# A hybrid attention, SSD and expert layer: the order of low parts, exponentials and output copies in attention, and the place of W_out's product

## The reference

```
x = x + attention(layernorm(x))     # 16 heads of 32, causal, softmax, Wo
x = x + experts(layernorm(x))       # 8 experts of rank 16, the best 2 by softmax gates
x = x + ssd(layernorm(x))           # below
x = x + experts(layernorm(x))       # the same weights

ssd(u):  proj = u @ W_in.T  -> xBC, z, A_log ; xBC = causal convolution of 4 taps over tokens + conv_b
         x, B, C = split(xBC) ; a = -softplus(A_log) ; L = exp(segsum(a))     # 32 heads of 16, state 64
         y = (C B^T * L) x + D x ; out = (y * silu(z + z_bias)) @ W_out.T
```

## Time and profile before

| | us |
|---|---|
| median of 3 runs (lowest, highest) | 3169.89 (3167.56, 3171.26) |
| the profiled execution, its time | 3168.84 |
| the profiled execution, its span | 3167.1 |

### The profile page before, as it was taken

How to read it: one execution, slowest core, us unless ns; L and a number is a source line. 1 busy time by engine, 2 the same in 40 slices (tenths; PEclk the granted TensorE clock), 3 DMA queues, 4 the chain that set the end, 5 groups by cost and what they waited for, 6 DMA issues and landing times.

```text
span 3167.1 us, 58505 instructions
## 1 busy us (share of the span) xinstructions
PE 2895.3 (91%) x20788; PEld 2064.0 (65%) x20788; DVE 1943.5 (61%) x2910; ACT 1181.2 (37%) x1877; POOL 696.5 (22%) x997
## 2 busy tenths in 40 slices
PE   3888989999898899999988889999989889999998
PEld 3655477777665457777765545777776544777776
DVE  2545465777745555677765556377776444647777
ACT  2244334444124423444323441444422443244442
POOL 3300012333210001333311001133322000023331
PEclk7999999999999999999999999999999999999999
DMA  9322011111232202111133220211123230111112
GB/s 342 84 60 65 18 52 49 46 50 47 82 73 59 58 14 54 46 48 49 41 94 74 48 48 14 67 49 48 38 68 88 48 78 18 42 50 51 46 45 77
DMA packets 163781, 192.03 MB, mean 61 GB/s; under 512 B 43963, under 2 KB 103995, under 8 KB 161787
## 3 DMA queue, kind: packets, MB, share of 16 engines
q1 hardware_dynamic: 156126, 175.57, 20.5%
q10 hardware_dynamic: 7456, 13.90, 1.4%
HBM read 106.99 MB, written 23.36 MB: 41 GB/s over the span
## 4 chain that ended last, share of the span: by engine, by line
PE 69%; DVE 13%; issue 8%; ACT 4%; SPq 3%; DMA 3%; POOL 1%; ACTq 1%; DVEq 0%; POOLq 0%
PE ps L745 14%; PE ps L746 13%; PE ps L747 13%; DVE mneg L1648 5%; PE ps L1110 4%; PE ps L993 3%; PE ps L923 3%; PE ps L866 3%; PE ps L1096 2%; PE ps L908 2%; PE ps L1119 2%; PE ps L1156 2%; PE ps L861 2%; ACT PR L1298 1%; DMA win_raw<-in_t 1%
## 5 line engine op out<-in xcount | busy, mean ns | idle before, releaser
L745 PE MATMUL ps<-uh,win 128*128 128x512 f32 x1536 | 625.4, 407 | 18.1 <-POOL win L1893 17.4
L746 PE MATMUL ps<-ul,win 128*128 128x512 f32 x1536 | 603.3, 393 | 0.0
L747 PE MATMUL ps<-uh,win 128*128 128x512 f32 x1536 | 602.0, 392 | 0.0
L1648 DVE TENSOR_REDUCE mneg<-ps 128x1 f32<-128x896 f32 (+7 forms) x512 | 366.9, 752 | 274.6 <-PE ps L866 273.1
L1298 ACT ACTIVATE PR<-ps 128x1024 f32<-128x1024 f32 (+3 forms) x384 | 293.3, 808 | 334.0 <-PE ps L908 307.2
L745 PEld LDWEIGHTS ps<-uh,win 128*128 128x128 f32 x1536 | 289.8, 189 | 92.8 <-POOL win L1893 19.8
L747 PEld LDWEIGHTS ps<-uh,win 128*128 128x128 f32 x1536 | 289.8, 189 | 64.9
L746 PEld LDWEIGHTS ps<-ul,win 128*128 128x128 f32 x1536 | 290.6, 189 | 53.8
L1762 DVE TENSOR_TENSOR LM<-ps,LM 128x512 f32<-128x512 f32 x256 | 170.2, 686 | 242.4 <-PE ps L1110 198.4
L1973 POOL TENSOR_SCALAR_AFFINE_SELECT LM<-LM 128x512 f32<-128x512 f32 x256 | 209.5, 830 | 491.4 <-ACT LM L1401 491.4
L923 PE MATMUL ps<-PR,V 128*32 128x512 f32 (+3 forms) x1536 | 285.9, 497 | 3.6 <-ACT PR L1298 2.3
(11 more groups left out here) (220 smaller groups left out, 5039.8 us busy)
## 6 DMA issues: line engine op xcount, KB each, us to landing
raw<-in_t SPq DMA_DIRECT2D x128, 256.0 KB, 2.8
QS<-EV SPq DMA_DIRECT2D x192, 128.0 KB, 2.5
KS<-EV SPq DMA_DIRECT2D x168, 128.0 KB, 2.6
in_t<-tiles ACTq DMA_DIRECT2D x10, 1024.0 KB, 9.2
XN<-in_L_attn_a_x_dram SPq DMA_DIRECT2D x40, 256.0 KB, 5.1
win_raw<-in_L_attn_a_Wqkv_dram SPq DMA_DIRECT2D x34, 256.0 KB, 3.4
win_raw<-in_t SPq DMA_DIRECT2D x32, 256.0 KB, 2.7
edec<-ed_t SPq DMA_DIRECT2D x512, 16.0 KB, 1.6
```

Of the source, the lines that this page charges most:

```text
L745: pe.matmul(dst, hi_l, hi_r, start=first, stop=False)
L746: pe.matmul(dst, hi_l, lo_r, start=False, stop=False)
L747: return pe.matmul(dst, lo_l, hi_r, start=False, stop=last)
L1648: dve.tensor_reduce(mneg[:, hh, t:t + 1], flat[:, off:off + (t + 1) * P], AX.X, ALU.max, negate=True).then_inc(a_max.sem, 1)
```

## The change

In attention, VectorE runs `project_lo` behind both groups of maxima of a session, not between them. ScalarE runs the exponentials of the next pair's units 0 and 1 ahead of `take(p, g, hf, 1)`. In a pair's first session TensorE issues the scores of units 2 and 3 one by one, each with its own wait. The load of W_out is issued after y of pair 13 is saved, ahead of pair 15's decays; its high part is made inside pair 14; the low part is split, half on VectorE inside pair 14 and half on GpSimd at the start of pair 15. The products of tiles 0 to 3 with k = 0 to 2 stand in four places inside the last pair (`fill`), those of tiles 5, 6, 4, 7 after it, each tile with a bank of its own; the parts k = 3 of all tiles come last. The last gate tile is done in two halves of tokens, each with a signal, and the last y is saved by SP and ScalarE, two transfers each. Ten matmuls of no use (`keep_awake`) stand behind the product.

```diff
@@ SP
-                    def save_y(j, q):
+                    def save_y(j, q, chunks):
...
-                        for c4 in range(4):
+                        for c4 in chunks:
...
-                                elif q == 2:
-                                    bc_pe.wait(sp, b * PAIRS + j, 2)
-                                    sp.dma_start(wout_raw, wout_dram.rearrange("p (k n) -> p k n", k=KT)).then_inc(s_wout, 16)
...
-                                save_y(j, q)
+                                save_y(j, q, range(2) if last and q == 3 else range(4))
+                                if last and q == 1:
+                                    bc_pe.wait(sp, b * PAIRS + j + 1, 2)
+                                    sp.dma_start(wout_raw, wout_dram.rearrange("p (k n) -> p k n", k=KT)).then_inc(s_wout, 16)
                                 if not (last and q >= 2):
                                     pair_decay(j + 2, q % 2)
@@ TensorE
                             if ahead:
                                 group_scores_a(p + 1, pair + 1, FILLING[k][0])
-                            scores_b(p, pair, (2 * k + 2, 2 * k + 3))
+                            if k == 0:
+                                scores_b(p, pair, (2,))
+                                scores_b(p, pair, (3,))
+                            else:
+                                scores_b(p, pair, (2 * k + 2, 2 * k + 3))
...
+                def product_part(t, k):
+                    t0 = t * P
+                    return three(ps[:, t, :], gh[:, k, t0:t0 + P], gl[:, k, t0:t0 + P], woh[:, k, :], wol[:, k, :], k == 0, k == KT - 1)
+
+                def product_start(t):
+
+                    for k in range(KT - 1):
+                        product_part(t, k)
...
+                    def fill(t):
+                        if ahead is None:
+                            if t == 0:
+                                gate.wait(pe, b, KT - 1)
+                                for i in range(2):
+                                    wout_lo[i].wait(pe, b, 1)
+                            if t == 2:
+                                bc_dve.wait(pe, n, 2)
+                            product_start(t)
...
                     segment(0)
                     project_ahead(0, 1)
+                    fill(0)
...
                     i.then_inc(ds_pe.sem, 1)
+                    fill(1)
                     inner(0)
                     segment(1)
...
                     project_ahead(1, 0)
+                    fill(2)
                     segment(2)
                     segment(3)
                     inner(1)
                     project_ahead(1, 1)
+                    fill(3)
...
-                wout_lo.wait(pe, b, 1)
-                row_product(lambda dst, k, t0, first, end:
-                            three(dst, gh[:, k, t0:t0 + P], gl[:, k, t0:t0 + P], woh[:, k, :], wol[:, k, :], first, end),
-                            b * 2 + 1, lambda: gate.wait(pe, b, KT - 1), lambda: gate.wait(pe, b, KT))
+                for t in (5, 6, 4, 7):
+                    if t == 4:
+                        y_dve.wait(pe, b * PAIRS + PAIRS - 1, 1)
+                    product_start(t)
+                for t in range(TT):
+                    if t % HALF == 0:
+                        gate.wait(pe, b, KT + t // HALF)
+                    product_part(t, KT - 1).then_inc(w_pe.sem, 1)
+                w_add.wait(pe, b * 2 + 1, 1)
+                keep_awake(0, 10)
+                w_add.wait(pe, b * 2 + 1, TT - 2)
@@ ScalarE
-                        take(p, g, hf, 1)
                         if ahead:
                             for u in range(2):
                                 exponentials(p + 1, u)
+                        take(p, g, hf, 1)
...
                     if later is not None:
                         pair_hi(n + 2, par, later)
+                    elif ahead:
+                        wout_split()
...
-                            if last and par == 0:
-                                wout_split()
                 value_hi(b + 1)
+                y_dve.wait(act, b * PAIRS + PAIRS - 1, 1)
+                for c4 in range(2, 4):
+                    act.dma_start(yt[3 * 32:4 * 32, :].rearrange("p (a c l) -> p a c l", a=2, c=4)[:, :, c4, :],
+                                  y1[c4 * 32:(c4 + 1) * 32, :, :]).then_inc(s_ysave, 16)
@@ VectorE
-                                    if g < GROUPS - 1 and k < 4:
-                                        project_lo(g + 1, k, False)
+                            if hf == 0 and g < GROUPS - 1 and k < 4:
+                                project_lo(g + 1, k, False)
...
                     if later:
                         pair_lo(n + 2, par)
+                    elif ahead:
+                        wout_hi.wait(dve, b, 1)
+                        dve.tensor_tensor(wol[:, 0:2, :], wout_raw[:, 0:2, :], woh[:, 0:2, :].bitcast(F32), ALU.subtract).then_inc(wout_lo[0].sem, 1)
...
-                            if last and q == 2:
-
-                                wout_hi.wait(dve, b, 1)
-                                dve.tensor_tensor(wol, wout_raw, woh[:, :, :].bitcast(F32), ALU.subtract).then_inc(wout_lo.sem, 1)
...
-                add_tiles(b * 2 + 1, w_pe, w_add, 0, b * 4 + 3, X)
+                add_tiles(b * 2 + 1, w_pe, w_add, 0, b * 4 + 3, X, banks=TT)
@@ GpSimd
+                    if final:
+                        pool.tensor_tensor(wol[:, 2:KT, :], wout_raw[:, 2:KT, :], woh[:, 2:KT, :].bitcast(F32), ALU.subtract).then_inc(wout_lo[1].sem, 1)
                     until(ya_pe, n, 0)
...
+                            if last and par:
+                                until(wout_hi, b, 1)
+                            mix(n, j, par, last and par)
```

More of the change, by code:

```diff
@@ L264, in hybrid_layer @@
         wout_hi = signal("wout_hi", 1)
-        wout_lo = signal("wout_lo", 1)
+        wout_lo = [signal(f"wout_lo{i}", 1) for i in range(2)]
         ln_var = signal("ln_var", 2)
@@ L366, in hybrid_layer @@
         s_zero = sem("s_zero")
-        gate = signal("gate", KT)
+        gate = signal("gate", KT + 1)
         SIGNALS_OF = {
-            "vector": [wout_lo, bcw_lo, ln_var, ln_xh, ln_lo, v_done, w_add, pj_lo, a_max, o_rec, z_dve, g_in, g_w, u_add,
+            "vector": [wout_lo[0], bcw_lo, ln_var, ln_xh, ln_lo, v_done, w_add, pj_lo, a_max, o_rec, z_dve, g_in, g_w, u_add,
                        al_dve, a_dve, cm_dve, cm_low, ed_in, xz_dve, bc_dve, scan, m_dve, y_mid, y_dve, gate],
@@ L373, in hybrid_layer @@
                        bt_act, cm_act, ed_act, ds_act, dt_act, seg_act],
-            "gpsimd": [wv_lo, qkw_lo, xzw_lo, ln_rstd, *o_scaled, cp_pool, xd_pool, xp_pool, sel_pool, st_pool],
+            "gpsimd": [wout_lo[1], wv_lo, qkw_lo, xzw_lo, ln_rstd, *o_scaled, cp_pool, xd_pool, xp_pool, sel_pool, st_pool],
             "tensor": [ln_tp, v_pe, w_pe, pj, a_pe, m_pe, st_pe, pv, z_pe, t_pe, u_pe, al_pe, dc_pe,
@@ L927, in weigh, with keep_awake @@
                     i.then_inc(pv.sem, 1)
-                def keep_awake(bank):
-                    for _ in range(4):
+                def keep_awake(bank, n=4):
+                    for _ in range(n):
                         pe.matmul(ps[:, bank, :], onesr[:, :], uh[:, 0, 0:HB], start=True, stop=True)
@@ L1496, in by_tile, with add_tiles @@
                         take(t - 1)
-            def add_tiles(n, product, added, bank, stats_of, src, loaded=None):
+            def add_tiles(n, product, added, bank, stats_of, src, loaded=None, banks=4):
                 for t in range(TT):
                     product.wait(dve, n, t + 1)
-                    dve.tensor_tensor(X[:, t, :], ps[:, bank + t % 4, :], X[:, t, :], ALU.add).then_inc(added.sem, 1)
+                    dve.tensor_tensor(X[:, t, :], ps[:, bank + t % banks, :], X[:, t, :], ALU.add).then_inc(added.sem, 1)
                     if t >= 1:
@@ L1798, in gate_tile, with tile @@
                     one = slice(m, m + 1) if isinstance(m, int) else bass.ds(m, 1)
-                    def tile(a):
-                        return a[:, one, :].rearrange("p a t -> p (a t)")
-                    xm, zm = tile(xT), tile(zs)
-                    at = (b * KT + m) * 3
-                    dve.scalar_tensor_tensor(xm, xm, dsk[:, one], yt, ALU.mult, ALU.add).then_inc(s_gate, 1)
-                    dve.wait_ge(s_gate, at + 1)
-                    dve.tensor_tensor(zm, xm, zm, ALU.mult).then_inc(s_gate, 1)
-                    dve.wait_ge(s_gate, at + 2)
-                    dve.sem_inc(s_tick, 1)
-                    dve.tensor_copy(tile(gh), zm).then_inc(s_gate, 1)
-                    dve.wait_ge(s_gate, at + 3)
-                    dve.tensor_tensor(tile(gl), zm, tile(gh).bitcast(F32), ALU.subtract).then_inc(gate.sem, 1)
+                    halves = 2 if isinstance(m, int) else 1
+                    for half in range(halves):
+                        tok = slice(half * L // halves, (half + 1) * L // halves)
+                        def tile(a):
```

(17 more changed lines are left out.)

## The result

| | before | after |
|---|---|---|
| median of 4 runs each, us | 3168.72 (3166.48 to 3171.26) | 3111.56 (3107.40 to 3118.52) |
| the profiled execution, its span | 3167.1 | 3110.5 |
| VectorE, share of the span | 61% | 62% |
| granted TensorE clock, mean | 0.977 | 0.980 |

The ratio is 0.9822, 95% interval [0.9802, 0.9841]: 57.2 us faster, where 50 to 51 were forecast. The time lies 7 us under the forecast and inside its range.

A forecast was written before the change was run, and what follows sets the result against it. TensorE was taken to bound the kernel, its idle time largely waits for VectorE's maxima. The terms 38.4 - 3.6 + 10.6 + 5.7 = 51.1 us gave 3118.5 us, 1.6% faster; range 3106 to 3142.

The forecast's parts named there:

- Low parts: Attention sessions: maxima start earlier with the low part behind them, 0.80 us at each of 48 waits, 38.4 us.
- stack copies: Attention: QS and KS copies, released later, make TensorE wait 0.9 us in the third group, 3.6 us cost in all.
- Exponentials and split: Attention's changes of pair: exponentials ahead of output copies, scores 2 and 3 apart; 2.6 us per image, 10.6 in all.
- step 2: Sign in attention: L904's waits for exponentials fall to some 5 us outside the last pair; output-copy waits stay small.
- W_out: Last SSD pair to expert logits: 36 matmuls moved inside the pair, some 2.7 us per image gained, 10.9 us before clock loss.
- step 3: W_out inside the last pair; signs: VectorE without gaps from first sum, 37 to 38 us to logits, half clock in first logits.
- The clock: First expert logits behind W_out: TensorE falls to half clock, 1.3 us lost per image, -5.2 us in all.
- A: Whole kernel: everything fits, stack copies land in time and the clock holds in the tail; 3110 us, chance 0.22.
- B: Attention: waits move to stack copies, an exponential or bank 7, losing half the low parts' gain; 3138 us, chance 0.11.
- C: Attention: maxima still released by something as late, so the low parts gain nothing; 3153 us, chance 0.05.
- D: Attention: late stack copies stall 12 places, 5 us each, making the kernel slower by 0.2% (6 us); chance 0.04.

The follow-up runs named there:

- wout_only: Kernel after with both attention edits undone, so only what concerns W_out is changed against the kernel before: 3162.02 us, ratio 0.9977 to before.
- order_only: Kernel before with exponentials 0 and 1 ahead of the second output copies (order alone), units 2 and 3 still together: 3161.21 us, ratio 0.9977.
- more_awake: Kernel after with 13 keep-awake matmuls, not 10, and ten fillers before the first expert logits behind W_out: 3106.83 us, 0.9814 to before; again 3105.48 us, 0.9804.
- awake_all: As more_awake, plus nine useless matmuls ahead of the first decay logits and eight behind the second experts: 3092.65 us, ratio 0.9769 to before.
- chunk3_early: Kernel after with chunk 3's low part back between the two maxima, the other three behind them: 3118.13 us, ratio 0.9844 to before.
- low_only: Kernel before with one edit, the low part behind both groups of maxima: 3127.30 us, ratio 0.9875.
- exps_split: Kernel before with order and split: exponentials 0 and 1 ahead of the copies, units 2 and 3 issued one by one: 3161.54 us, ratio 0.9982.

## Why the prediction was right, step by step

**Low parts.** Forecast 38.4 us, less 3.6 for the stacks. Between "order and split" and "after" the table shows 3.15, 3.17 and 3.48 us for the three pairs with projections, 9.8 us for twelve waits, 0.82 each; 39.2 us in four images, less 1.3 for the copies: 37.9. (The third pair gains 0.3 more because one of its four waits was 1.25 us long before, not the 0.94 to 0.99 that I had read for all; the others gave 0.79 each.) The reasoning was right in each link: VectorE started the low part while scores lay ready, and what became late (bank 7, the next maximum) had the room that the rows gave it. The mis-sized term of these two is the **stack copies**: I let the slow triple of issues of the earlier trace rows (1.25 us over the others) reach the needed copy in each of four images, and took 2.6 us to land. In the kernel after a slow triple stands there in three images, the copy of 289.6 was used 2.5 us later at 292.07, and the price was 1.3 us. Elsewhere the estimate held: issued 0.63 us behind session 4's scores (226.97 to 227.60; I said 0.7), no wait.

**Exponentials and split.** Forecast 10.6 us, 2.6 an image (the terms written there add up to 10.4); measured 1.9, which is 7.7 us. This is the term that was most wrong in its links. By the interval that ends at the change, the gain into the pairs without projections is 0.35 where I had 0.33, which agrees with the bound by the first maximum. Into those with projections I took the whole wait of 0.7 for gained and got 0.45, since exponential 0 can start only when its own scores are there; the 0.36 us left is that. Into the last pair I had 0 and it lost 0.46, into g = 3 I had 0 and it gained 0.44. The first pair's split, for which I had 0.2, gave 0.09 (interval 2, order alone against both). L904's waits for exponentials were forecast at some 5 us outside the last pair and are 11.8 in all, 0.94 at each last change, so 8 outside: this sign of step 2 did not come.

**Both together.** 38.4 - 3.6 + 10.6 = 45.4 us were forecast. With the half-clock stretches taken out (below) attention gained 45.7. The closeness is luck: the copies cost 2.3 us less and the low parts gave 0.8 more than forecast, and the exponentials gave 2.9 less.

**W_out.** Forecast 10.9 us and measured 11.1. By link: y later by 1.95, measured 2.13; the first sum later by 1.01, measured 1.19; VectorE's chain from it to the low part 11.05, measured 10.86 (799.34 to 810.20); the stage 36.55, measured 36.47. That VectorE becomes the bound shows in its timeline, which has no gap there, and in the 36.5 us that the stage takes in every kernel with the fills, with and without keep-awake matmuls and fillers. W_out's load and the two halves of its low part, which I had costed at nothing, cost nothing: the load is issued 15.4 us ahead of the pair (759.06), as forecast, the first batch starts 1.14 us behind the pair's first matmul (775.60), and the SSD up to this pair takes as long as before.

One sign that I had written down misleads. I wrote that 37 to 38 us would show step 3 right and that under 36.8 us would mean that the clock held. My own sum gave 36.55, and the stage took 36.47 with the clock at half in the first logits: its loss lies behind the stage, and the length of the stage can't show it.

**The clock.** Forecast -5.2 us, measured -5.7 (and -6.0 in wout_only). Of the 5.7, 1.2 is not the clock's: the first masks of image 1 wait 2.09 us for stack copies instead of 0.94. Such waits of 2 us and more come in some images of other kernels too (three in order_only, none in wout_only), and so not from this change; wout_only is the cleaner figure. Here the traces and the Trainium skill (TensorE: Matmul & The Clock Gate, Part 1: The HAM clock gate) could be read either way: it says that activity releases the full rate, and I had weighed that the ten keep-awake matmuls would be that activity. The runs agree with the page and with the row: matmuls in the sparse stretch itself held the clock (1.00 in more_awake and, at the decay logits, in awake_all), and ten ahead of it only put the fall off, from inside the stage to the logits, and gained nothing that can be measured (3113.31 against 3111.56 us, within the intervals).

**What the forecast had not counted.** Its terms explain 45.7 + 11.1 - 5.7 = 51.1 us. That this is also the forecast's sum is luck, as the terms show. The rest of the 56.6 is 3.3 us in attention and 3.7 at the decay logits, less 1.5 ahead of the first attention, where the change does nothing and the spans differ from run to run (120.2 to 124.5 us). The 3.3 and the 3.7 go with stretches of 3.4 us at half clock. Attention has three of them before and one after; the intervals give the price of each, 38.95 against 37.29 in the sixth, 16.15 against 14.61 in the last: 1.5 to 1.7 us. One execution's share of them is partly chance: in the two profiled runs of more_awake the decay stage of image 2 takes 81.95 (0) and 83.82 (6.2). Whether shorter waits make them rarer is open. Of the images of kernels with the low parts in their old place 11 of 16 have at least one in attention, of those with the new place 10 of 28; but the four of chunk3_early, with one old wait in four, all do. No run here settles it. The interval of the ratio (50 to 63 us) holds the forecast's 51 as well, so the difference of 6 us is read from the two traces and not from the medians.

The rivals: A (everything fits, 3110) came close in time, but its reason is half wrong, since the copies fitted but for 1.3 us and the clock did not hold. B and C fell with low_only. D needed 5 us at each of 12 places, and the most was 0.6. The time of 3118.5 us has a slip of 0.3: 3117.7 and 1.1 are 3118.8.

## What to carry to other kernels

Look in the trace for an engine that does deferrable work between two steps that another engine waits for, and put the work behind the second: here 48 times 0.8 us, with the slack of what becomes late read off first. Work moved into a chain's gaps pays only partly (8.4 us moved, 2.8 won an image), because each piece delays the chain and the next engine becomes the bound. Where TensorE waited for VectorE ahead of a dense stretch, useless matmuls in that very wait won back what the half clock cost there, and ahead of it they won nothing.

## What the runs showed of the hardware

From the first attention on the half clock came in stretches of 3.4 to 10.2 us, and one of 3.4 us in attention costs 1.3 to 1.7 us (26.68 against 25.37 in interval 8 of exps_split, 38.95 against 37.29 in interval 6 of before). They were cheap to avoid: three batches of eight to ten matmuls of no use, some 2 us each and in time that TensorE waited anyway, with three more keep-awake matmuls, won 17 us of 3111 (0.9822 to 0.9769; 16.8 in the two stages of the traces). I had not expected the clock's loss in stages that the change does not touch to be larger than the one it causes. Nor had I expected the program to repeat so exactly: without such a stretch or a late copy the same interval agrees within 0.05 us from image to image (but for image 0's third) and between kernels with the same code there, so the traces separate 0.5 us an image that the medians could not.
